# Attention and a mixture of experts on one core: the scatters of a batch spread between the splits of q and k, the filling reordered, and the rows of maxima issued ahead of a wait

## The reference

```
# attention: 16 heads of 8, rank 8; zq = q V, zk = k V, zv = v V
att = softmax(einsum('bhqr,bhkr->bhqk', zq, zk) / sqrt(rank))
y   = einsum('bhqk,bhkr->bhqr', att, zv) @ U.T          # back to 128 columns
x   = layernorm(x + y @ Wo.T + bo)
# experts: 8 of them, hidden 512, each row goes to its best two
p   = softmax(x @ gate_w.T); the two best, their weights scaled to a sum of 1
h   = relu(einsum('td,ehd->teh', x, w1) + b1)
out = sum over the two chosen e of weight * (einsum('teh,edh->ted', h, w2) + b2)
x   = layernorm(x + out)
```

## Time and profile before

| | us |
|---|---|
| three runs | 1251.39, 1258.94, 1264.15 |
| median | 1258.94 |
| the profiled execution | 1257.38 |
| its span in the profile | 1255.6 |
| first stage until its last scatter | about 940 |
| mean granted TensorE clock | 0.939 of full speed |

### The profile page before, as it was taken

One profiled execution on the slowest core, in us unless ns is written; L12 is line 12 of the kernel. 1 busy time (PEld: TensorE's weight loads), 2 busy tenths in 40 slices (PEclk: granted clock), 3 DMA queues, 4 the chain that ended last, 5 costly groups with the idle time before them and its releaser, 6 DMA issues. The chain is left out here.

```text
span 1255.6 us, 24757 instructions
## 1 busy us (share of the span) xinstructions
PE 1082.8 (86%) x7711; PEld 520.5 (41%) x7711; DVE 975.3 (78%) x2117; ACT 904.2 (72%) x1177; POOL 586.5 (47%) x823
## 2 busy tenths in 40 slices
PE   3578998989889898898988999888728999999977
PEld 2222222222222222222222222222218999999952
DVE  4578888989778797887988879797146888888845
ACT  1157877778677786867878678687618999999927
POOL 1314316255271642626336263323254777777745
PEclk9989999999899998989999899899758999999989
DMA  3733133141331413223142231400012222222246
GB/s 80 235 94 90 49 101 89 54 132 42 95 92 51 126 37 106 73 67 102 43 127 69 71 97 36 122 15 19 14 51 63 69 68 69 69 69 71 66 159 257
DMA packets 105461, 104.88 MB, mean 84 GB/s; under 512 B 21608, under 2 KB 82834, under 8 KB 105376
## 3 DMA queue, kind: packets, MB, share of 16 engines
q1 hardware_dynamic: 94912, 81.88, 22.5%
q0 software_dynamic: 8448, 16.93, 4.2%
q10 hardware_dynamic: 2016, 4.98, 1.1%
HBM read 56.06 MB, written 47.39 MB: 82 GB/s over the span
## 5 line engine op out<-in xcount | busy, mean ns | idle before, releaser
L799 DVE TENSOR_REDUCE row_max<-score_ps 128x2 f32<-128x1024 f32 x512 | 618.0, 1220 | 138.9 <-PE score_ps L571 91.3
L685 ACT ACTIVATE probs<-score_ps 128x1024 f32<-128x1024 f32 x512 | 521.6, 1023 | 157.4 <-PE score_ps L553 132.6
L534 PE MATMUL av_ps<-probs,v_one 128*9 128x512 f32 x2048 | 285.2, 630 | 7.9 <-ACT probs L685 6.5
L571 PE MATMUL score_ps<-k_stack,q_stack 48*128 48x512 bf16 x1024 | 207.5, 402 | 75.2 <-ACT probs L685 57.5
L553 PE MATMUL score_ps<-q_stack,k_stack 51*128 51x512 bf16 x1024 | 205.7, 399 | 22.0 <-DVE row_max L799 15.1
L371 POOL TENSOR_TENSOR max_parts<-neg_max,zeros 32x128 bf16<-32x128 f32 x32 | 14.2, 445 | 386.9 <-ACT neg_max L623 386.9
L1096 ACT ACTIVATE w_cur<-experts 128x1156 f32 x136 | 158.5, 1167 | 37.5 <-PEq L413 17.2
L553 PEld LDWEIGHTS score_ps<-q_stack,k_stack 51*128 51x128 bf16 x1024 | 49.2, 93 | 320.4 <-issue 154.2
L1192 POOL DMA_INDIRECT y_d<-y_out,place x136 | 136.8, 1006 | 44.7 <-issue 44.7
L846 POOL DMA_INDIRECT routed_d<-rows,slot_i x128 | 125.4, 980 | 67.2 <-issue 36.9
L1053 PE MATMUL up_ps<-xt_sb,w_cur 128*128 128x128 f32 x1088 | 146.2, 278 | 0.0
(11 more groups left out here) (187 smaller groups left out, 1153.3 us busy)
## 6 DMA issues: line engine op xcount, KB each, us to landing
k_stack<-k_stack_d SPq DMA_DIRECT2D x128, 96.0 KB, 2.4
q_stack<-q_stack_d SPq DMA_DIRECT2D x128, 96.0 KB, 2.5
x_rows_sb<-routed_d SPq DMA_DIRECT2D x136, 65.0 KB
q_stack_d<-q_parts SPq DMA_DIRECT2D x32, 192.0 KB
k_stack_d<-k_parts SPq DMA_DIRECT2D x30, 192.0 KB
x_in<-L_attn_x SPq DMA_DIRECT2D x16, 256.0 KB, 3.1
q_stack_d<-q_parts SPq DMA_DIRECT2D x32, 128.0 KB
x_res<-L_attn_x SPq DMA_DIRECT2D x16, 256.0 KB, 3.1
```

What stands on the lines that cost most here:

```text
L534: last = nc.tensor.matmul(av_ps[32 * g:32 * g + V_COLS, :], v_one[n.parity][:, kb, HG * hg + g, :], probs[:, (2 * j + g // 2) % P_RING, g ...
L571: last = nc.tensor.matmul(max_bank(b, s)[:, a, :], q_stack[n.parity][at, c, g * P:(g + 1) * P], k_stack[n.parity][at, c, :], start=True, s ...
L685: nc.scalar.activation(probs[:, s % P_RING, :, :], exp_bank(b, s)[:, :, :], ACT.Exp).then_inc(S["exp_done"], 1)
L799: nc.vector.tensor_reduce(row_max[:, m // (STEPS // 2), :, m % (STEPS // 2)], max_bank(b, s)[:, :, :], AX.X, ALU.max).then_inc(S["red_done ...
```

## The change

It consists of four parts.

1. **POOL's order in a body.** The first two scatters come ahead of `split_max(b, 1)`, the next two behind it. In bodies with `prev2`, `cur` and `proj` (2 to 13) the last four are placed one by one: between the second and third operation of the split of q, behind that split, between the second and third operation of the split of k, and behind that. `split` takes a function `between` for it. `split_max(n1, 0)` of such a body comes last. Body 14 and 15 have scatters 4 to 7 in a row ahead of it.
2. **SP's order.** `max_rows(n1, 0)` moves from behind the wait for the stores and the first eight loads of the stacks to ahead of that wait.
3. **The filling.** The experts stand at steps 24 to 31, one a step. The transposes of w1 and of w2 are two groups with a semaphore increment each, and each waits only for the copy of its own half. In body -1 the maxima of batch 0 are split between q and k on POOL, and their rows issued between the stores of q and of k on SP.
4. **SCALE_AT** goes from 16 to 17: `scale_out` stands at steps 18 to 21.

```diff
@@ -34,8 +34,8 @@
 STORES = 2 * (len(Q_PLACES) + len(K_PLACES))
 
 
-EXPERT_AT = [STEPS - 2 * (E - e) for e in range(E)]
-SCALE_AT = 16
+EXPERT_AT = [STEPS - E + e for e in range(E)]
+SCALE_AT = 17
 LEAST = -3.0e38
 
 class Batch:
@@ -366,26 +366,28 @@
             LOADS = 4 * 16
             MAX_LOADS = 2 * 3 * 16
 
-            def split(engine, queue, full, parts, rest_t, zeros, part_ready, value, last_sem):
+            def split(engine, queue, full, parts, rest_t, zeros, part_ready, value, last_sem, between=None):
 
                 engine.tensor_tensor(parts[:, 0, :], full, zeros, ALU.add).then_inc(part_ready, 1)
                 queue.wait_ge(part_ready, value(1))
                 engine.tensor_tensor(rest_t, full, parts[:, 0, :], ALU.subtract).then_inc(part_ready, 1)
+                if between:
+                    between()
                 queue.wait_ge(part_ready, value(2))
                 engine.tensor_tensor(parts[:, 1, :], rest_t, zeros, ALU.add).then_inc(part_ready, 1)
                 queue.wait_ge(part_ready, value(3))
                 engine.tensor_tensor(parts[:, 2, :], rest_t, parts[:, 1, :], ALU.subtract).then_inc(last_sem, 1)
 
-            def split_q(engine, queue, n):
+            def split_q(engine, queue, n, between=None):
                 queue.wait_ge(S["q_sb"], n.count(1, 1))
                 wait(queue, S["parts_stored"], n.count(16 * STORES, 0))
                 wait(queue, S["split_done"], n.count(2, 0))
-                split(engine, queue, q_f[:, :], q_parts, rest[:, :], zeros[:, :], S["qpart_ready"], lambda k: n.count(3, k), S["split_done"])
-
-            def split_k(engine, queue, n):
+                split(engine, queue, q_f[:, :], q_parts, rest[:, :], zeros[:, :], S["qpart_ready"], lambda k: n.count(3, k), S["split_done"], between)
+
+            def split_k(engine, queue, n, between=None):
                 queue.wait_ge(S["k_sb"], n.count(1, 1))
                 queue.wait_ge(S["split_done"], n.count(2, 1))
-                split(engine, queue, k_f[:, :], k_parts, rest[:, :], zeros[:, :], S["kpart_ready"], lambda k: n.count(3, k), S["split_done"])
+                split(engine, queue, k_f[:, :], k_parts, rest[:, :], zeros[:, :], S["kpart_ready"], lambda k: n.count(3, k), S["split_done"], between)
 
             def store_parts(queue, stack_d, parts, places):
                 for part, first, count, stride in places:
@@ -579,9 +581,12 @@
                         def transpose_expert(e):
                             if e == 0:
                                 pe.wait_ge(experts_loaded, 32)
+                            wait(pe, experts_copied, 2 * e - 1)
+                            for h in range(HB):
+                                last = nc.tensor.transpose(score_ps[2][:, 0, h * P:(h + 1) * P], w1_n[:, e * HB + h, :], ident[:, :])
+                            last.then_inc(experts_ps, 1)
                             wait(pe, experts_copied, 2 * e)
                             for h in range(HB):
-                                nc.tensor.transpose(score_ps[2][:, 0, h * P:(h + 1) * P], w1_n[:, e * HB + h, :], ident[:, :])
                                 last = nc.tensor.transpose(score_ps[2][:, 1, h * P:(h + 1) * P], w2_n[:, e, h * P:(h + 1) * P], ident[:, :])
                             last.then_inc(experts_ps, 1)
 
@@ -623,8 +628,9 @@
                             nc.scalar.activation(neg_max[half][:, :], misc_ps[0:HALF, 0:P], ACT.Copy, scale=-1.0).then_inc(S["negmax_sb"], 1)
 
                         def copy_expert(e):
-                            act.wait_ge(experts_ps, e + 1)
+                            act.wait_ge(experts_ps, 2 * e + 1)
                             nc.scalar.activation(experts[:, e, W1], score_ps[2][:, 0, :], ACT.Copy).then_inc(experts_copied, 1)
+                            act.wait_ge(experts_ps, 2 * e + 2)
                             nc.scalar.activation(experts[:, e, W2], score_ps[2][:, 1, :], ACT.Copy).then_inc(experts_copied, 1)
 
                         for s in range(STEPS):
@@ -856,14 +862,16 @@
                             wait(pool, S["res_ready"], p1.count(1, 0))
                             nc.gpsimd.tensor_tensor(x_bo[:, :, :], x_res[p1.parity][:, :, :], bo_b[:, :].unsqueeze(1).to_broadcast([P, QT, D]),
                                                     ALU.add).then_inc(S["xbo_ready"], 1)
-                        if cur:
-                            split_max(b, 1)
                         if prev2:
                             pool.wait_ge(S["place_out"], p2.count(1, 1))
                             pool.wait_ge(S["top_step"], p2.count(TOP_STEPS, TOP_STEPS))
                             pool.wait_ge(S["slot_step"], p2.count(SLOT_STEPS, SLOT_STEPS))
                             pool.wait_ge(S["copied"], p2.count(1, 1))
                             scatter(p2, 0, 2)
+                        if cur:
+                            split_max(b, 1)
+                        if prev2 and cur:
+                            scatter(p2, 2, 4)
                         if prev:
                             pool.wait_ge(S["mv_ready"], p1.count(QT, QT))
                             nc.gpsimd.tensor_tensor(var_eps[:, :], mean_var[:, :, 1], eps_t[:, :], ALU.add).then_inc(S["vareps_ready"], 1)
@@ -874,15 +882,22 @@
                             pool.wait_ge(S["minus_ready"], p1.count(1, 1))
                             pool.wait_ge(S["rstd_ready"], p1.count(1, 1))
                             nc.gpsimd.tensor_tensor(shift[:, :], minus_mean[:, :], rstd[:, :], ALU.mult).then_inc(S["shift_ready"], 1)
+                        spread = prev2 and cur and proj
+                        if prev2 and cur and not proj:
+                            scatter(p2, 4, 8)
                         if proj and not is_first(b):
-                            split_q(nc.gpsimd, pool, n2)
-                            split_k(nc.gpsimd, pool, n2)
-                        if prev2:
-                            scatter(p2, 2, 6)
-                        if nxt:
+                            split_q(nc.gpsimd, pool, n2, (lambda: scatter(p2, 4, 5)) if spread else None)
+                            if not cur:
+                                split_max(n1, 0)
+                            if spread:
+                                scatter(p2, 5, 6)
+                            split_k(nc.gpsimd, pool, n2, (lambda: scatter(p2, 6, 7)) if spread else None)
+                            if spread:
+                                scatter(p2, 7, 8)
+                        if cur and nxt:
                             split_max(n1, 0)
-                        if prev2:
-                            scatter(p2, 6, 8)
+                        if prev2 and not cur:
+                            scatter(p2, 2, 8)
 
                     schedule(pool, body)
 
@@ -924,16 +939,18 @@
                         if proj:
                             sp.wait_ge(S["split_done"], n2.count(2, 1))
                             store_parts(sp, q_stack_d[n2.parity], q_parts, Q_PLACES)
+                        if nxt and not cur:
+                            max_rows(n1, 0)
                         if proj and not is_first(b):
                             sp.wait_ge(S["split_done"], n2.count(2, 2))
                             store_parts(sp, k_stack_d[n2.parity], k_parts, K_PLACES)
+                        if cur and nxt:
+                            max_rows(n1, 0)
                         if proj:
                             sp.wait_ge(S["parts_stored"], n2.count(16 * STORES, 16 * STORES))
                             wait(sp, S["st_done"], b.count(STEPS, 2 * GROUP) if cur else 0)
                             stacks(n2, 0)
                             stacks(n2, 1)
-                        if nxt:
-                            max_rows(n1, 0)
                         if proj:
                             wait(sp, S["st_done"], b.count(STEPS, 3 * GROUP) if cur else 0)
                             stacks(n2, 2)
```

## The result

The changed kernel takes 1184.54 us (median of four runs, 1182.83 to 1190.66) beside 1261.18 us for the kernel before (1251.39 to 1264.15): a ratio of 0.941, 95% interval 0.935 to 0.948. The profiled execution took 1184.38 us, 73.0 less than that of before; 50.2 were forecast.

What follows compares the result with a forecast made beforehand. It took DVE as pace-setter, delayed by late PE results and half clock. Gains of 43.8 (scatters), 0.9 (body 1) and 5.5 (filling) sum to 50.2 us, taken from 1257.38: 1207 us, range 1196 to 1240.

Steps and rivals of the forecast that it cites:

- The stall and its half clock: Steps 24 to 25: late PE results cost some 2 us at once, then matmuls at half clock; 3 to 6 us a body.
- the stall needs the burst of scatters and the burst of stores together: At the stores of k: four scatters in a row must meet six stores; spreading the scatters removes some 2 us plus half clock.
- the 43.8 us: Gain forecast from spreading the scatters in the twelve full bodies: 12 x (52.85 - 49.2).
- the size of a body without the stall: Full bodies: the 50.80 us interval at clock 1.00, less 1.6 us of late starts, gives 49.2 us.
- Nothing, and I see no more than 1 us either way: SCALE_AT one step later and the order in the last bodies: no gain forecast, at most 1 us either way.
- The floor of 48.10 a body: Body 14's interval, with scatters but no splits or stores of q and k, taken as the lower bound for a body.
- This edit pays for the other one: Rows of maxima ahead of the stores' wait: left behind it, the later stores would make them 3.6 us later.
- the rival on these rows: Rows of maxima become last; PE waits 1 to 2 us at step 0: 11 us lost, 1218; no chance of its own.
- no longer last: Filling: rows of maxima issued by 69 us, so the first matmul of the exponentials, at 70.8, would not wait for them.
- part of the stall stays: Rival, 20%: one scatter beside the stores still holds PE's results about 1 us a body; 1233 us.
- move to the later stores: Rival, 10%: the wait moves to the later stores of k, steps 27 to 28; only the filling gains; 1251 us.
- double: Rival, 8%: two waits of some 2 us, at the stores of q and of k, each with half clock; 1296 us.

Runs made afterwards that it cites:

- the rows put back: Kernel after, with the first half's rows of maxima issued again behind the stores' wait and the loads of the stacks: 1267.5 us.
- the row of four back: Kernel after, with the last four scatters again in one row behind the split of k, beside the stores of k: 1250.3 us.
- the early rows: Kernel after, with scatters 2 to 5 in a row behind split_max(b, 1), beside six small rows of maxima, and 6 and 7 behind the split of k: 1203.7 us.
- three and three: Kernel before, with scatters three ahead of and three behind the split of the maxima's first half, not four and two: 1238.4 us; with rows of maxima early, 1236.6 us.

## Why the prediction was right and wrong

**The stall and its half clock: the mechanism stood, its cause was too narrow.** That the hold at step 25 goes with the spread, and the half clock with it, is shown by the kernel after (step 24 at 1.90, clock 1.00) and by the row of four that brings both back. Of the 4.9 us by which a body became shorter, 1.9 are step 24, 2.7 steps 26 to 29 behind it, and 0.3 step 16. But "the stall needs the burst of scatters and the burst of stores together" was wrong in its second half. I had read the DMA engines falling idle as DVE restarted as the cause; a row of four beside six small rows holds PE's results at a share of 0.2 too, and one beside nothing of SyncE for 1 us. Body 1, with no scatters and no late result, is evidence for the scatters. Body 14 was no evidence for the stores: between 0.54 and 1.63 us after the start of its last scatter no result of PE ends, and the one at 1.63 is 0.20 late. Its row of four happens to stand where little can be held.

By the rule of the Trainium skill in "Trainium Architecture — The Big Picture", section "What this means for kernel authors", engine lanes and DMA ports cannot contend; the prediction said that the rows speak against it. The runs take that back: dense traffic is not needed to hold the results. The conclusion drawn from the rule, that the 43.8 us would not come, was wrong all the same, since the hold exists and follows the scatters.

**The failed step: the size of a body without the stall.** It said "Taking away 1.6 us of it ... leaves 49.2"; it is 47.95, and 12 x 1.25 = 15.0 of the 22.8 us that the sum fell short. The interval of 50.80 held more than the stall: step 24 is 1.6 us too long in it, and that is all I subtracted. The rest, by its steps beside those of after, is 0.3 at step 16, which SCALE_AT removed, and 0.9 in steps 28 to 31, 0.6 of it in the last, where the next body's first matmul starts. Late rows of maxima would do that. In body 1 they did: with the rows alone early its step 31 takes 1.06 us instead of 2.26. In a full body the profile puts the wait down to DVE, and no run separates it at a clock of 1.00. "Nothing, and I see no more than 1 us either way" for SCALE_AT was wrong by itself: 0.34 in each body, 4.7 us between the medians. I had looked at whether its reader was late, not at the step it left.

**The floor was none.** "The floor of 48.10 a body" was body 14 of the kernel before, with SCALE_AT = 16 and a last step of 1.9 us itself; body 14 now takes 47.44. A body of the kernel that one changes contains what the change removes, so it bounds nothing from below. The range's lower end, 1192 and then 1196, was worked out from it.

**The rows of maxima.** "This edit pays for the other one" was right, and the estimate of 3.6 us later is 4.0 (44.1 to 48.1 into the body). But no price was put on its absence, and the rival on these rows was priced at 11 us. Measured, it is 83 us: 1267.5 against 1184.5. "I take nothing" for PE's wait held, with little margin: with the row of four ahead of the split of q the rows go out 1.3 to 4.2 us later, and the bodies are 0.6 to 3.5 us longer, so the margin is some 0.7 us, an estimate from these bodies.

**The filling** was sized at 5.5; the two profiles give 6.9 and the run of its own 9.7 (5 to 14). The first matmul pair of the exponentials starts at 69.60 where 70.8 was forecast, and still waits for the rows of maxima, which "no longer last" denied:

```profile
69.60 0.39 PE L555 MATMUL score_ps<-q_stack,k_stack 51*128 51x512 bf16 x2 [1.10 <-DMA q_stack<-max_parts]
```

**Bodies 0 and 1** gave 3.9 instead of 0.9: 1.5 in body 1, as its wait for the rows and step 16 went, 1.7 in body 0, and 0.7 in the first steps of body 2, which began at half clock in the kernel before. Body 0's part goes with the filling, for a reason that stays open: of the fifteen kernels with the new filling thirteen have a body 0 of 45.9, the one with the filling alone among them, and the five with the old one 47.5 to 49.4. The other two, with the rows put back and with SCALE_AT = 16, have 47.4 and 47.5. **The end** gave 3.4 where nothing was forecast; 0.7 of it is body 14. Another 2.1 lie in body 15, from its step 10 to its last exponential, and are luck: that stretch takes 33.4 before and 31.3 after, but 29.9 to 34.3 among kernels that differ from after only in other bodies.

**The rivals.** One scatter beside the stores holds next to nothing, 0.32 us at most in three bodies of the twelve ("part of the stall stays", 20%); the stall did not move to the later stores (10%) nor double (8%). A partial stall does exist, at 1190 to 1203 us, but by the place of a row, and the change leaves no row of more than two in bodies 2 to 13.

## What to carry to other kernels

Two moves in one change can be worth nothing alone and everything together: where a hold is removed, look up what it was covering, and price the change with and without the second move. To size a stage without its stall, subtract step by step against the same step elsewhere, and take no part of the old kernel as a floor. Where a body without the stall is to be evidence, look whether anything could have been held in it. Before blaming traffic that ends when a wait ends, put the same row of instructions where that traffic isn't.

## What the runs showed of the hardware that was not expected

**A row of scatters holds PE's semaphore increments.** The trace records when semaphores are raised. In the twelve bodies of every kernel, the increments of ACT, DVE and GpSimd that are recorded follow the end of their instruction within 0.02 us. Those of PE do not, behind three or four scatters on GpSimd that start 1.3 us apart: in body 6 of the kernel before, the pair of matmuls with a modelled end at 423.47 raises its semaphore at 425.56, and DVE, which waits for it, starts at 425.58. The profile's "remote" stands for such an increment here. ACT's and DVE's readers start late though PE goes on.

Late are above all the results that end from some 0.6 us after the start of the row's last scatter on. Of those that end 0.6 to 1.7 us after it, in the twelve bodies, this many were over 0.3 us late:

| row | late | by at most, us |
|---|---|---|
| 4, beside DMAs of SyncE (eight kernels) | 130 of 130 | 1.65 |
| 4, ahead of the split of q | 13 of 23 | 1.04 |
| 3 | 156 of 173 | 1.48 |
| 2 | 24 of 405 | 0.82 |

Results that end earlier, during the row, are held at times too, and longest: by up to 2.9 us. Single scatters came to 0.32.

The last of the held readers restarts 2.1 to 2.4 us after the start of the row's last scatter, which itself takes 0.96: at 425.58 after 423.30 in the kernel before, 419.19 after 417.05 with the row of four back, 396.81 after 394.61 beside the stores of q, 385.29 after 382.94 beside the early rows, 414.52 after 412.28 behind the split of the maxima. ACT's copy of the product is let go earlier in the first two, at 424.81 and 417.80.

```profile
412.28 0.96 POOL L852 DMA_INDIRECT routed_d<-rows,slot_i  x1 [0.31 <-issue]
414.52 1.23 DVE L805 TENSOR_REDUCE row_max<-score_ps 128x2 f32<-128x1024 f32 x1 [0.88 <-remote]
```

The share of the DMA engines was between 0.04 and 0.97 in these cases. With no DMAs of SyncE beside it, ahead of the split of q, the hold ends 1.7 to 1.8 us after that start. The Trainium skill says in "Perfetto Trace Analysis", section "DMA Instruction — SWDGE (GPSIMD)", that such an instruction's end in the profile is the writing of its last descriptor, not the end of its transfer. The DMA records of the traces agree, and a hold that lasts about until the row's transfers are through fits them: in the kernel before the row's last packet ends at 425.38, beside the early rows at 384.82, 0.2 and 0.5 us before the restart; ahead of the split of q it ends at 391.5, 0.1 us behind the late increment of 391.42. No run shows that the transfers are the cause. Why PE's increments alone are held, and why pairs hardly hold any, stays open.

The granted clock fell behind waits of PE of 2.38 to 2.97 us in ten of the twelve bodies of the kernel before, behind 1.44 to 1.76 us in eight of twelve with three and three, and behind 1.13 to 1.56 us in one of twelve beside the stores of q. The length of the wait alone does not decide it. A hold costs 1.4 us a body without the half clock behind it and 5.7 with it.
